# A fused two-layer gated transformer block on one core: token-tile attention, 512-column query products and a reordered head

## The chip, the cores and the metric

The kernel runs on one core of a Trainium2 chip. The metric is the device time of one execution in microseconds (us), the median of several runs. Five engines work side by side: PE (matrix multiply; its weight loads are shown as PEld), DVE (vector), ACT (scalar activation functions), POOL (GpSimd) and SP, which here only starts the transfers. They order their work by semaphores: each engine has one queue and stops at a wait until another engine has counted high enough.

## What is computed

x is [4, 256, 512] (1024 tokens of width 512), the context is [4, 64, 512]. Cut to what matters:

```python
x = x + tanh(g_xattn[0]) * xattn0(layernorm(x), ctx)   # 32 query heads, 8 key heads, keys: the 64 context rows
x = x + tanh(g_ffn[0])   * ffn0(layernorm(x))          # SiLU gate, inner width 1376
x = x + tanh(g_xattn[1]) * xattn1(layernorm(x), ctx)   # 32 query heads, 8 key heads, q and k RMS-normalised
x = x + tanh(g_ffn[1])   * ffn1(layernorm(x))          # dense base + top-2 of 28 rank-8 experts
# xattn1(latents, context):
kv = concat([context, latents], axis=1)                # 64 + 256 = 320 keys
q = rms_norm(heads(latents @ Wq), q_norm_w); k = rms_norm(heads(kv @ Wk), k_norm_w); v = heads(kv @ Wv)
out = softmax(q @ k.T / sqrt(128)) @ v                 # per head of width 128
return heads_joined(out) @ Wo
```

## The kernel before

**Split products.** Each fp32 operand is held as a rounded part (`_hi`) and a remainder (`_lo`), and every product is three matmuls: hi x lo, lo x hi, hi x hi (`mm3`, L55 to L59, so most PE rows carry L57, L58 or L59). Each result that is used again leaves PSUM in two steps: ACT writes the rounded part, DVE subtracts it from PSUM for the remainder.

**Stages.** The program runs one after the other: a head (L312 and on, until about 38 us in), `attn0_phase` over 8 key-head groups, `ffn0_phase`, `attn1_phase` over 8 groups, and inside its `tail` the last feed-forward stage. The head loads the context (`ctxT`), the first key-value, query and output weights (`raw_kv`, `raw_q`, `raw_o`), splits them (DVE rounds and subtracts, L332 to L352; POOL does the context remainder and four pieces of the output weight remainder), makes the keys and values (`kv` preps), the products of keys and query weights (`wk` preps) and the layer norm of eight token tiles (DVE statistics, POOL reciprocal root, ACT `act_norm`, PE transpose `pe_turn`, ACT `act_hi`, DVE `dve_lo`). After it POOL splits the next group's key-value weights (`split_kv`) before it first scales attention weights, and PE transposes those.

**Second attention.** A unit is one key head with its four query heads (group g, 0 to 7) and one batch row b (0 to 3): 32 units, n = 4 g + b. Each engine has the loop over b written out by hand in `body`. For unit n PE makes, in this order, keys and values (`kv_proj`, two token tiles), for even b the context's keys and values of two batch rows (`cx`), then for the unit before, u = n - 1, the products of attention weights and values (`p_v`) and transposes (`turn`), and for n the query product (`q_proj`), the transposes of k and q, the scores in four pieces, and the output product of u (`out`). PSUM has two bank pairs for this, by turns (`x_bank`, `y_bank`), so a product often waits until DVE has read the bank's former content: `p_v` of an even b waits for `kv_split`, the query product of an even b for `cx_split`.

In the query product the output tile is two heads of both token tiles: 256 columns a matmul. `PAIRS` gives the order of the score pieces. On DVE, `kv_lo` does the remainder of v (L1082), for b = 0 two pieces of the query weight remainder for this group (L1015), the remainder of the context's v (L1091) and the sums of squares of k (L1097), from which POOL makes the scale that `k_raw` gets at L1117 (`k_scaled`); `t_lo` of piece 2 (L1026) stands ahead of it.

**Late layer-norm tiles.** Six token tiles of a layer norm are made within units 1, 30 and 31 (`ln_tiles`), because x is complete only then. `turn_2` transposes the second of a pair and then piece 2 of the attention weights, which waits for `dve_lo` of the first.

## Time and profile before

| | |
|---|---|
| median of 3 runs | 1440.13 us (1435.58 to 1440.22) |
| the profiled execution | 1438.7 us, of it span 1436.9 us |
| PE busy | 1385.1 us (96%), 8744 matmuls |
| DVE busy | 1042.7 us (73%) |
| ACT busy | 796.3 us (55%) |
| POOL busy | 501.3 us (35%) |
| mean granted PE clock | 0.990 of full speed |

The span runs from the first to the last instruction; the rest of the execution's time lies around it. Matmuls overlap in the records, so a busy PE is not a measure of how fast it works: the distance from one start to the next is.

### The profile page before, as it was taken

To read this page: it belongs to the slowest core of one execution; us is meant where nothing else is said; L and a number is where in the kernel's file an instruction comes from. 1 tells how busy PE (TensorE), PEld (TensorE's weight loads), DVE (VectorE), ACT (ScalarE), POOL (GpSimd) and SP (SyncE) were. 2 spreads that over 40 slices of the span, in tenths; PEclk is the share of its full clock that TensorE was granted. 3 is DMA by queue.
4 is the path that set the end of the run, shared out by engine and by line. 5 is a ranking of instruction groups with operands and counts; after the bars stand their busy time and mean duration, and the time that the engine had idled before them with its cause. 6 is when DMAs were issued, how large, how long until landed. Compare 5 with 4: busy or idle time off the path is not lost.

```text
span 1436.9 us, 25319 instructions
## 1 busy us (share of the span) xinstructions
PE 1385.1 (96%) x8744; PEld 1240.6 (86%) x8744; DVE 1042.7 (73%) x2730; ACT 796.3 (55%) x2210; POOL 501.3 (35%) x623
## 2 busy tenths in 40 slices
PE   4999999999999998999999999999999999999998
PEld 4899989987778877899899999999999999999877
DVE  7777787787623435777787787787787777778775
ACT  4787787774211304565565565565555556556631
POOL 3965565654955512221212212222122221222220
PEclk9999999999999998999999999999999999999999
DMA  5211222211321300100100101001001001000001
GB/s 198 74 62 56 73 73 73 73 59 59 105 59 49 123 1 1 74 1 1 74 1 4 70 0 58 15 0 73 0 0 73 0 0 73 15 31 14 1 8 52
DMA packets 14944, 63.86 MB, mean 44 GB/s; under 512 B 1760, under 2 KB 1760, under 8 KB 10656
## 3 DMA queue, kind: packets, MB, share of 16 engines
q1 hardware_dynamic: 14880, 63.07, 12.5%
q8 instruction: 32, 0.52, 0.2%
q14 instruction: 32, 0.26, 0.1%
HBM read 60.97 MB, written 2.10 MB: 44 GB/s over the span
## 4 chain that ended last, share of the span: by engine, by line
PE 52%; DVE 6%; ACT 3%; issue 1%; POOL 0%; ACTq 0%
PE psum L57 15%; PE psum L58 14%; PE psum L59 14%; PE psum L1393 3%; PE psum L1406 2%; PE psum L1432 2%; ACT p L1256 1%; DVE pT_lo L1022 1%; DVE mx L1059 1%; ACT pT_hi L1231 1%; DVE pT_hi L1026 1%; PE psum L1388 1%; DVE p L1075 1%; PE psum L1509 1%; DVE v_lo L1082 0%
## 5 line engine op out<-in xcount | busy, mean ns | idle before, releaser
L1256 ACT ACTIVATE p<-psum,nb,rq 128x320 f32<-128x320 f32 x256 | 155.3, 614 | 154.5 <-DVE nb L1063 154.5
L57 PE MATMUL psum<-w1q_hi,xnT_lo 128*128 128x256 f32 (+1 forms) x544 | 163.0, 300 | 0.0
L59 PE MATMUL psum<-w1q_hi,xnT_hi 128*128 128x256 f32 (+1 forms) x544 | 157.3, 289 | 0.0
L58 PE MATMUL psum<-w1q_lo,xnT_hi 128*128 128x256 f32 (+1 forms) x544 | 157.1, 289 | 0.0
L982 POOL TENSOR_TENSOR p<-p,rinv 128x640 f32<-128x640 f32 x64 | 80.2, 1254 | 206.0 <-DVE rinv L1069 206.0
L1059 DVE TENSOR_REDUCE mx<-psum 128x2 f32<-128x640 f32 x128 | 104.7, 818 | 4.5 <-PE psum L59 4.5
L1231 ACT ACTIVATE pT_hi<-psum 128x512 fp32r<-128x512 f32 x128 | 69.7, 596 | 66.0 <-PE psum L1393 66.0
L1022 DVE TENSOR_TENSOR pT_lo<-psum,pT_hi 128x512 fp32r<-128x512 f32 x128 | 85.3, 687 | 27.7 <-ACT pT_hi L1231 25.9
L59 PEld LDWEIGHTS psum<-w1q_hi,xnT_hi 128*128 128x128 f32 x544 | 103.8, 191 | 1.3
L57 PEld LDWEIGHTS psum<-w1q_hi,xnT_lo 128*128 128x128 f32 x544 | 104.1, 191 | 1.1
L58 PEld LDWEIGHTS psum<-w1q_lo,xnT_hi 128*128 128x128 f32 x544 | 104.1, 191 | 1.0
L58 PE MATMUL psum<-w1o_lo,oT_hi 128*128 128x512 f32 x256 | 100.3, 392 | 0.0
L57 PE MATMUL psum<-w1o_hi,oT_lo 128*128 128x512 f32 x256 | 100.3, 392 | 0.0
L59 PE MATMUL psum<-w1o_hi,oT_hi 128*128 128x512 f32 x256 | 99.8, 390 | 0.0
L370 DVE TENSOR_TENSOR VW_lo<-psum,VW_hi 64x512 fp32r<-64x512 f32 x128 | 88.0, 688 | 14.5 <-ACT VW_hi L462 12.8
L57 PE MATMUL psum<-kT_hi,qT_lo 128*128 128x320 f32 x256 | 86.5, 338 | 2.3 <-DVE qT_lo L1053 2.1
L57 PE MATMUL psum<-w_kv_hi,xnT_lo 128*128 128x256 f32 x288 | 86.0, 299 | 1.8 <-PEq L692 1.8
L1046 DVE CUSTOM_DVE_ANT_0 dump<-q_raw 128x128 f32<-128x128 f32 x256 | 59.5, 288 | 34.5 <-ACT q_raw L1244 34.5
L1244 ACT ACTIVATE q_raw<-psum 128x512 f32<-128x512 f32 x64 | 38.2, 597 | 82.5 <-PE psum L59 82.4
L58 PE MATMUL psum<-w_kv_lo,xnT_hi 128*128 128x256 f32 x288 | 83.0, 288 | 0.0
L59 PE MATMUL psum<-w_kv_hi,xnT_hi 128*128 128x256 f32 x288 | 82.9, 288 | 0.0
L995 POOL TENSOR_TENSOR rq<-ssq,rms_eps 128x8 f32<-128x8 f32 x32 | 6.4, 200 | 218.8 <-DVE ssq L1046 218.8
(236 smaller groups left out, 4707.9 us busy)
## 6 DMA issues: line engine op xcount, KB each, us to landing
raw_q<-in_w0q SPq DMA_DIRECT2D x8, 1024.0 KB, 4.8
raw_o<-in_w0o SPq DMA_DIRECT2D x8, 1024.0 KB, 4.7
raw_q<-in_w1q SPq DMA_DIRECT2D x8, 1024.0 KB, 7.5
raw_o<-in_w1o SPq DMA_DIRECT2D x8, 1024.0 KB, 4.8
raw_kv<-in_w_gu SPq DMA_DIRECT2D x10, 512.0 KB, 3.6
raw_gu<-in_w_gu SPq DMA_DIRECT2D x10, 512.0 KB, 3.6
raw_kv<-in_w0kv SPq DMA_DIRECT2D x8, 515.0 KB, 3.3
raw_kv<-in_w1kv SPq DMA_DIRECT2D x8, 512.0 KB, 5.5
```

The lines of the kernel that those rows point to most:

```text
L57: pe.matmul(out, w[1], m[0], start=start, stop=False)
L58: pe.matmul(out, w[0], m[1], start=False, stop=False)
L59: return pe.matmul(out, w[0], m[0], start=False, stop=stop)
L370: last = dve.tensor_tensor(k.VW[1][r, h // 2, 2 * pr + bp, :], bank[64 * bp:64 * bp + 64, :], f(k.VW[0][r, h // 2, 2 * pr + bp, :]), ALU.s ...
L982: pool.tensor_tensor(p, p, k.rinv[:, stat(j)].unsqueeze(2).to_broadcast([PART, 2, KEYS]), ALU.mult).then_inc(p_scaled_pool, 1)
L1022: last = dve.tensor_tensor(k.pT[1][:, kt, 2 * hp:2 * hp + 2, :], bank.rearrange("p (h q) -> p h q", h=2), f(k.pT[0][:, kt, 2 * hp:2 * hp + ...
L1046: last = dve.tensor_tensor_reduce(k.dump[:, 4 * hp + i, :], q, q, 1.0, 0.0, ALU.mult, ALU.add, k.ssq[:, 4 * hp + i:4 * hp + i + 1])
L1059: dve.tensor_reduce(k.mx[:, stat(j)], s_pair(j), AX.X, ALU.max).then_inc(mx_ready, 1)
L1231: last = act.activation(k.pT[0][:, kt, 2 * hp:2 * hp + 2, :], bank.rearrange("p (h q) -> p h q", h=2), ACT.Copy)
L1244: act.activation(k.q_raw[:, hp, :], y_bank(b, "q", hp, alone)[:, :], ACT.Copy).then_inc(q_copied, 1)
L1256: last = act.activation(k.p1[:, tile, 2 * hp + hh, :], s_pair(j)[:, hh, :], ACT.Exp, bias=k.nb[:, i:i + 1], scale=k.rq[:, i:i + 1], accum_ ...
L1393: last = pe.transpose(bank[:, (2 * hh + tile) * PART:(2 * hh + tile + 1) * PART], k.p1[:, tile, 2 * hp + hh, CTX * hh + kt * PART:CTX * hh ...
```

## The change

- **Second attention by token tile.** The tiles of q, of the attention weights and of their product with v are laid out as [token tile, four heads] in place of [two heads, both tiles]. `q_proj` now makes four heads of one token tile: 12 matmuls of 512 columns in place of 24 of 256. `PAIRS` goes through the two head pairs of tile 0 first. `out` waits for its own tile's product alone.
- **Even units on DVE.** `kv_lo` is taken apart. For even b the remainder of v comes ahead of `t_lo` piece 2; then the sums of squares of k (which wait for a new semaphore, `kc_copied`), for b = 0 the two query weight pieces, and last the remainder of the context's v.
- **Unit 0.** The second query product stands behind the transposes of k; the keys and values of b = 1 are made in two halves around score piece 2, and score piece 3 stands ahead of the transposes.
- **Layer-norm units and tail.** The second late tile is transposed between the two halves of `kv_proj`, and piece 2 of the attention weights behind the second half; ACT does `act_hi` of the first tile ahead of the exponentials of piece 3. In the tail `pe_ag(0)` and `pe_base(0)` move ahead.
- **Head.** ACT rounds the key-value and query weights in pieces, DVE subtracts piece by piece and also does the context remainder; POOL rounds the output weights, the first piece between layer-norm tiles 6 and 7. The `wk` preps run over c for the first head pair and then for the second, one tile ahead of the transposes. The load of `bo` moves behind all others, `gates` and `normw` behind the query weights.

```diff
@@ second attention, views and PE
-    PAIRS = [(0, 0), (1, 0), (0, 1), (1, 1)]
+    PAIRS = [(0, 0), (0, 1), (1, 0), (1, 1)]
...
-            def q_proj(n, b, hp, alone=False):
-                for tile in range(2):
-                    t = 2 * b + tile
-                    for c in range(CH):
-                        last = mm3(pe, y_bank(b, "q", hp, alone)[:, tile * 256:(tile + 1) * 256],
-                                   [w[:, c, t * PART:(t + 1) * PART] for w in k.xnT],
-                                   [w[:, c, hp * 256:(hp + 1) * 256] for w in k.w_q], c == 0, c == CH - 1)
+            def q_proj(n, b, tile, alone=False):
+                t = 2 * b + tile
+                for c in range(CH):
+                    last = mm3(pe, y_bank(b, "q", tile, alone)[:, :], [w[:, c, t * PART:(t + 1) * PART] for w in k.xnT],
+                               [w[:, c, :] for w in k.w_q], c == 0, c == CH - 1)
                 last.then_inc(q_full, 1)
...
+                kv_half(b, 0)
+                late = ln_tiles(u)
+                if prev and not late:
+                    turn(u, b, 2)
+                if prev and late:
+                    pe.wait_ge(t_split, 6 * u + 2)
+                    ln.pe_turn(pe, *late[1], ln_bank(b - 1, 1))
+                kv_half(b, 1)
+                if prev and late:
+                    turn(u, b, 2, late=late[0])
...
                     if prev:
                         pe.wait_ge(t_split, 6 * u + 4)
-                    else:
-                        pe.wait_ge(cx_split, 1)
-                        q_proj(n, b, 1, True)
                     pe.wait_ge(k_scaled, n + 1)
...
+                    else:
+                        pe.wait_ge(cx_split, 1)
+                        q_proj(n, b, 1, True)
                     q_turn(n, b, 0, not prev)
...
                     if not prev:
-                        kv_proj(g, 1, False, False)
+                        kv_half(1, 0)
...
                     if prev:
                         out(u, b, 1)
+                    else:
+                        kv_half(1, 1)
+                        scores(n, b, 3)
                     turn(n, b, 0)
                     turn(n, b, 1)
-                    scores(n, b, 3)
+                    if prev:
+                        scores(n, b, 3)
...
             def tail(n):
                 u = n - 1
-                turn_2(u, 0)
+                late = ln_tiles(u)
                 ffn1.pe_ag(pe, 0)
+                pe.wait_ge(t_split, 6 * u + 2)
+                ln.pe_turn(pe, *late[1], ln_bank(BATCH - 1, 1))
+                turn(u, 0, 2, late=late[0])
+                ffn1.pe_base(pe, 0)
@@ second attention, DVE body
+                    if b % 2 == 0:
+                        v_lo(g, b)
+                    if prev:
                         t_lo(u, b, 2)
+                    if b % 2 == 1 and not (first and b == 1):
+                        v_lo(g, b)
                     if not (first and b == 1):
-                        kv_lo(g, b, first)
+                        k_squares(g, b)
+                    if b == 0 and not first:
+                        w_lo("q", g, 2)
+                        w_lo("q", g, 3)
+                    if b % 2 == 0:
+                        cx_lo(g, b)
                     if prev:
                         t_lo(u, b, 3)
                         t_lo(u, b, 4)
@@ head, DVE
-        head_kv()
-        head_q()
-        dve.wait_ge(in_small, 48)
+        dve.wait_ge(ctx_hi, 1)
+        dve.tensor_tensor(k.ctxT[1][:, :], k.xn_tok[:, :, :].rearrange("p a b -> p (a b)"), f(k.ctxT[0][:, :]),
+                          ALU.subtract).then_inc(ctx_lo, 1)
+        dve.wait_ge(kv_in, 16)
+        bias_copy(dve).then_inc(bias_in, 1)
+        for i in range(CONV["kv"]):
+            head_kv_lo(i)
+        head_q_row()
+        for h in range(3):
+            head_q_shift(h)
+        head_q_lo(0)
+        head_q_shift(3)
+        head_q_lo(1)
+        prep(None, ("kv", 0))
+        stats(0)
+        head_q_lo(2)
+        head_q_lo(3)
@@ head, POOL
         for t in range(NT):
             ln.pool_rstd(pool, 0, t)
-        for i in range(CONV["o"]):
+            if t == 6:
+                pool.wait_ge(o_in, 16)
+                hi_piece("o", 0)
+                lo_piece("o", 0, 0)
+        for i in range(1, CONV["o"]):
+            hi_piece("o", i)
             lo_piece("o", 0, i)
```

Where DVE starts a unit with b = 0 of groups 1 to 7, its queue before holds these rows (pT is the transposed attention weights, v_lo 128x256 the remainder of v, v_lo 64x128 that of the context's v, ssk the sums of squares of k, w1q the query weights):

```order
L1026 TENSOR_TENSOR pT_hi<-psum,pT_hi 64x256 x2
L1082 TENSOR_TENSOR v_lo<-psum,v_hi 128x256
L1015 TENSOR_TENSOR w1q_lo<-raw_q,w1q_hi 128x512 x2
L1091 TENSOR_TENSOR v_lo<-psum,v_hi 64x128 x4
L1097 ISA dump,ssk<-k_raw 128x128
...
L1022 TENSOR_TENSOR pT_lo<-psum,pT_hi 128x512 x2
```

And now, with the new kernel's line numbers:

```order
L1118 TENSOR_TENSOR v_lo<-psum,v_hi 128x256
L1065 TENSOR_TENSOR pT_hi<-psum,pT_hi 64x2x128 x2
L1125 ISA dump,ssk<-k_raw 128x128
...
L1054 TENSOR_TENSOR w1q_lo<-raw_q,w1q_hi 128x512 x2
L1133 TENSOR_TENSOR v_lo<-psum,v_hi 64x128 x4
L1061 TENSOR_TENSOR pT_lo<-psum,pT_hi 128x512 x2
```

The remainder of v has moved to the front; the remainder of the context's v, which frees the bank of the query product, now stands behind the squares as well as behind the query weight pieces.

In the head, DVE's queue before up to the first statistics of x (ln_st):

```order
L419 CAST ctxT_hi<-xn_tok 128x1024
L206 COPY bias<-raw_kv 128x6
L332 CAST w_kv_hi<-raw_kv 128x1024
L334 TENSOR_TENSOR w_kv_lo<-raw_kv,w_kv_hi 128x1024
L209 TENSOR_SCALAR q_last<-raw_q 128x4
L341 COPY raw_q<-bias 128x4
L343 TENSOR_SCALAR raw_q<-raw_q,q_last 128x511 x4
L346 CAST w0q_hi<-raw_q 128x2048
L348 TENSOR_TENSOR w0q_lo<-raw_q,w0q_hi 128x2048
L425 SCALAR_TENSOR_TENSOR qkw<-normw 128x1
L360 SCALAR_TENSOR_TENSOR kvT_lo<-psum,bias,kvT_hi 128x256 x2
L91 BN_STATS ln_st<-x 128x6
```

And now:

```order
L418 CAST ctxT_hi<-xn_tok 128x1024
L420 TENSOR_TENSOR ctxT_lo<-xn_tok,ctxT_hi 128x1024
L207 COPY bias<-raw_kv 128x6
L335 TENSOR_TENSOR w_kv_lo<-raw_kv,w_kv_hi 128x512 x2
L210 TENSOR_SCALAR q_last<-raw_q 128x4
L342 COPY raw_q<-bias 128x4
L345 TENSOR_SCALAR raw_q<-raw_q,q_last 128x511 x3
L351 TENSOR_TENSOR w0q_lo<-raw_q,w0q_hi 128x512
L345 TENSOR_SCALAR raw_q<-raw_q,q_last 128x511
L351 TENSOR_TENSOR w0q_lo<-raw_q,w0q_hi 128x512
L359 SCALAR_TENSOR_TENSOR kvT_lo<-psum,bias,kvT_hi 128x256
L91 BN_STATS ln_st<-x 128x6
```

Both big casts have left this queue, half of the query remainder and the second kvT_lo stand behind the first statistics, and the context remainder has come in.

## Rows read from the trace of the kernel before

**Rows 1.** The page, its first line.

```profile
span 1436.9 us, 25319 instructions
```

**Rows 2.** Stretches: us, busy time by engine, granted PE clock, DMA share, GB/s.

```profile
549.50:556.30 6.80, 6.18 (x27) 5.79 (x26) 4.43 (x13) 2.97 (x8) 1.85 (x2) 0.50 0.00 0
751.00:803.00 52.00, 51.73 (x348) 47.45 (x349) 41.06 (x123) 30.16 (x80) 10.77 (x12) 1.00 0.13 51
```

**Rows 3.** Timeline of PE, unit 10: start, length, what; query and output product.

```profile
805.31 0.28 PE L58 MATMUL psum<-w1q_lo,xnT_hi 128*128 128x256 f32 x1
...
807.95 0.28 PE L59 MATMUL psum<-w1q_hi,xnT_hi 128*128 128x256 f32 x1
...
815.97 0.39 PE L57 MATMUL psum<-w1o_hi,oT_lo 128*128 128x512 f32 x1
...
818.48 0.39 PE L59 MATMUL psum<-w1o_hi,oT_hi 128*128 128x512 f32 x1
```

**Rows 4.** Timeline at the start of unit 12 (b = 0), last row unit 10.

```profile
852.42 0.86 DVE L1026 TENSOR_TENSOR pT_hi<-psum,pT_hi 64x256 fp32r<-64x256 f32 x2
852.48 0.38 ACT L1270 ACTIVATE v_hi<-psum 128x256 fp32r<-128x256 f32 x1
853.31 0.42 DVE L1082 TENSOR_TENSOR v_lo<-psum,v_hi 128x256 fp32r<-128x256 f32 x1
853.65 1.28 DVE L1015 TENSOR_TENSOR w1q_lo<-raw_q,w1q_hi 128x512 fp32r<-128x512 f32 x2
853.86 0.49 PE L57 MATMUL psum<-pT_hi,v_lo 128*128 128x512 f32 x1 [0.27 <-DVE v_lo L1082]
854.95 1.20 DVE L1091 TENSOR_TENSOR v_lo<-psum,v_hi 64x128 fp32r<-64x128 f32 x4
856.17 0.29 DVE L1097 CUSTOM_DVE_ANT_0 dump<-k_raw 128x128 f32<-128x128 f32 x1
856.60 0.36 PE L57 MATMUL psum<-w1q_hi,xnT_lo 128*128 128x256 f32 x1
...
803.46 1.20 DVE L1091 TENSOR_TENSOR v_lo<-psum,v_hi 64x128 fp32r<-64x128 f32 x4 [1.22 <-ACT v_hi L1276]
```

**Rows 5.** Timeline ahead of the scores of unit 10.

```profile
813.28 0.69 DVE L1053 TENSOR_TENSOR qT_lo<-psum,qT_hi 128x512 fp32r<-128x512 f32 x1
814.12 0.39 PE L57 MATMUL psum<-kT_hi,qT_lo 128*128 128x320 f32 x1
```

**Rows 6.** Timeline in unit 0 and at the start of unit 1.

```profile
541.73 1.20 DVE L1091 TENSOR_TENSOR v_lo<-psum,v_hi 64x128 fp32r<-64x128 f32 x4 [1.87 <-ACT v_hi L1276]
...
549.12 0.83 PE L1432 MATMUL psum<-ident,q_raw 128*128 128x128 f32 x4 [2.22 <-DVE kT_lo L1136]
...
564.65 0.79 PE L57 MATMUL psum<-pT_hi,v_lo 128*128 128x512 f32 x1 [0.84 <-DVE pT_lo L1022]
```

**Rows 7.** Timeline of PE behind units 30 and 31: turns of piece 2 and of the late tile.

```profile
1343.68 0.44 PE L1388 MATMUL psum<-ident,p 128*128 128x128 f32 x2 [1.04 <-DVE xnT_lo L132]
...
1370.58 0.66 PE L120 MATMUL psum<-ident,xn_tok 128*128 128x128 f32 x4 [1.28 <-DVE pT_lo L1022]
```

**Rows 8.** Timeline of the head and the first steps behind it.

```profile
10.96 0.17 DVE L209 TENSOR_SCALAR q_last<-raw_q 128x4 f32<-128x4 f32 x1 [1.58 <-DMA raw_q<-in_w0q]
...
14.35 2.29 DVE L348 TENSOR_TENSOR w0q_lo<-raw_q,w0q_hi 128x2048 fp32r<-128x2048 f32 x1
...
17.41 0.69 DVE L91 BATCH_NORM_STATS2 ln_st<-x 128x6 f32<-128x512 f32 x1
...
34.95 5.06 POOL L246 TENSOR_TENSOR w0o_lo<-raw_o,w0o_hi 128x512 fp32r<-128x512 f32 x4 [2.09 <-DVE w0o_hi L352]
...
36.58 0.68 DVE L365 TENSOR_TENSOR WK_lo<-psum,WK_hi 128x512 fp32r<-128x512 f32 x1
...
43.76 0.64 POOL L295 TENSOR_TENSOR p<-p,rinv 128x256 f32<-128x256 f32 x1
44.45 0.44 PE L575 MATMUL psum<-ident,p 128*128 128x128 f32 x2 [0.37 <-POOL p L295]
```

More of the change, by code:

```diff
@@ L160, in attn0_phase @@
     LN_TILES = 4
-    HEAD_ORDER = [("kv", 0), ("kv", 1)] + [("wk", j) for j in range(8)] + [("vw", 0, 0)]
+    HEAD_WK = [("wk", 2 * c + hp) for hp in range(2) for c in range(CH)]
+    HEAD_ORDER = [("kv", 0), ("kv", 1)] + HEAD_WK + [("vw", 0, 0)]
     CONV = {"kv": 2, "q": 4, "o": 4}
@@ L535, in prep @@
                     pe.wait_ge(prep_free, place(base, ("kv", 0))[0] + 1)
-                    pe.wait_ge(q_lo, CONV["q"] * (g + 1))
+                    if base is not None:
+                        pe.wait_ge(q_lo, CONV["q"] * (g + 1))
+                if base is None and c == 0:
+                    pe.wait_ge(q_lo, 2 * hp + 2)
                 for h in range(2):
@@ L931, in p_pair, with shared @@
         return k.p1[:, tile, 2 * hp:2 * hp + 2, :].rearrange("p h n -> p (h n)")
+    def shared(w, tile, half, i):
+        return w[halves[half], 2, tile, i:GH:2, :]
     def stat(j):
@@ L1076, in scale_p, with v_lo @@
                 last.then_inc(p_scaled, 1)
-            def kv_lo(g, b, first):
-                n = BATCH * g + b
-                dve.wait_ge(kv_hi, n + 1)
+            def v_lo(g, b):
+                dve.wait_ge(kv_hi, BATCH * g + b + 1)
                 bank = y_bank(b, "kv")[:, :].rearrange("p (t n) -> p t n", t=2)
@@ L1083, in kv_lo, with k_squares @@
                                   ALU.subtract).then_inc(kv_split, 1)
-                if b == 0 and not first:
-                    w_lo("q", g, 2)
-                    w_lo("q", g, 3)
+            def k_squares(g, b):
                 if b % 2 == 0:
-                    dve.wait_ge(cx_hi, 2 * g + b // 2 + 1)
-                    for i in range(2):
-                        for half in (slice(0, 64), slice(64, PART)):
-                            last = dve.tensor_tensor(k.v[1][half, b + i, 2, :],
-                                                     y_bank(b, "cx")[64 * i:64 * i + 64, HD:2 * HD],
-                                                     f(k.v[0][64 * i:64 * i + 64, b + i, 2, :]), ALU.subtract)
-                    last.then_inc(cx_split, 1)
-                nk = 3 if b % 2 == 0 else 2
-                for i in range(nk):
+                    dve.wait_ge(kc_copied, 2 * g + b // 2 + 1)
+                for i in range(3 if b % 2 == 0 else 2):
                     last = dve.tensor_tensor_reduce(k.dump[:, 2 * GH + i, :], k.k_raw[:, i, :], k.k_raw[:, i, :], 1.0, 0.0,
@@ L1099, in kv_lo, with cx_lo @@
                 last.then_inc(ssk_ready, 1)
+            def cx_lo(g, b):
+                dve.wait_ge(cx_hi, 2 * g + b // 2 + 1)
+                for i in range(2):
+                    for half in (slice(0, 64), slice(64, PART)):
+                        last = dve.tensor_tensor(k.v[1][half, b + i, 2, :],
+                                                 y_bank(b, "cx")[64 * i:64 * i + 64, HD:2 * HD],
+                                                 f(k.v[0][64 * i:64 * i + 64, b + i, 2, :]), ALU.subtract)
+                last.then_inc(cx_split, 1)
             def body(g, first, nxt):
@@ L1154, in body @@
                     scale_p(n, 1)
+                    row_max(n, 2)
                     if not prev:
-                        kv_lo(g, 1, first)
-                    row_max(n, 2)
+                        v_lo(g, 1)
+                        k_squares(g, 1)
                     if prev:
@@ L1460, in kv_proj @@
                     pe.wait_ge(x_added, 2 * (u - 1) + 1)
-                for tile in range(2):
-                    t = 2 * b + tile
-                    for c in range(CH):
-                        last = mm3(pe, y_bank(b, "kv")[:, tile * 256:tile * 256 + 256],
-                                   [w[:, c, t * PART:(t + 1) * PART] for w in k.xnT],
-                                   [w[:, c, :] for w in w_kv3], c == 0, c == CH - 1)
-                    if tile == 0 and prev:
-                        turn_2(u, b)
-                last.then_inc(kv_full, 1)
+                kv_half(b, 0)
[8 more added lines that the diff above has]
+                    turn(u, b, 2, late=late[0])
             def body(g, first, nxt):
@@ L1478, in body @@
                     else:
-                        turn_2(u, b)
+                        turn(u, b, 2)
                     if deep:
```

255 lines of the change are left out of this document (127 added, 128 removed).

## Prediction

> **What bounds the kernel now.** I read the page first: PE is busy 96% of a span of 1436.9 us [rows 1], so a change counts only by what it takes from PE's own work, or from PE's waits. The windows next: in 52 us of the steady second attention PE is busy for 51.73 at full clock, the other engines for less; near the start of that stage there are 6.8 us at half the clock [rows 2]. PE works at two levels there, 2.4 GHz and 1.2 GHz, and each microsecond of full-clock work done at the lower one costs a second one. Last came the timeline, for the places at which PE waits: for DVE at the start of each even unit [rows 4], in unit 0 and at the start of unit 1 [rows 6], behind the late layer-norm tiles and in the tail [rows 7], and all through the head, whose end is a chain of DVE, POOL and PE [rows 8]. Ahead of the scores nothing is shown as a wait, but little is missing: the second q remainder starts at 813.28 with 0.69 of work, and the scores start 0.2 later than its end [rows 5]. The sum below is made against the profiled execution's own 1438.7 us, which is 1.4 below the median of the runs shown (1440.13).
>
> **Query products.** From the first to the last of 24 matmuls of 256 columns is 22 steps of the printed rows, 2.64 us, so 0.120 each; the out product's 512-column ones go 2.51 us in 11 steps, 0.228 each [rows 3]. A q product is thus 24 x 0.120 = 2.88 before and 12 x 0.228 = 2.74 now, 0.14 less. There are 64 of them. Those of units 30 and 31 meet waits for the layer norm, and unit 0 is counted below, so 60 x 0.14 = **-8.4**. The bounds: 0, if the gain only turns into waits (a rival below), and 9.0 for all 64. The transposes, scores and output products keep their shapes.
> The Trainium skill, "TensorE: Matmul & The Clock Gate", section "Back-to-back issue gap", gives an isolated matmul of N columns N/2.4 + 2.5 ns, by which dropping half the matmuls saves only the 2.5 ns of each of the 768 dropped, 1.9 us. By that rule the q term would be 1.9 us instead of 8.4. The trace does not agree with so small a fixed part: its rows [rows 3] fit one of about 12 ns.
>
> **Even units, b = 2.** p_v waits for the remainder of v. ACT's v_hi ends at 852.86, but DVE is in t_lo piece 2 until 853.28 and does the remainder at 853.31; the matmul comes at 853.86 with 0.27 of idle shown [rows 4]. With v_lo ahead of t_lo piece 2 the remainder can start 0.45 earlier; the idle by the modelled ends is 0.27, so the gain lies between these, and I take 0.4, since the modelled end of the matmul before lies behind its real share. The context's remainder is late by nothing: in unit 10 it stands after 1.22 us of idle for ACT's v_hi [rows 4], and t_lo (0.86) goes before that idle anyway, while three squares of about 0.25 fit into it. Seven of eight such units have the wait: 7 x 0.4 = **-2.8** (1.9 to 3.2).
>
> **Even units, b = 0, groups 1 to 7.** The same 0.4 is gained at p_v, but what is late next is the q product, which waits for the context's remainder (it frees the bank). DVE after v_hi's end at 852.86 now has v_lo 0.42, t_lo piece 2 0.86, three squares 0.72, two query weight pieces 1.28, and the context's remainder 1.20 [rows 4]: 4.48, so it ends at about 857.35, and q can't start before 857.4. It started at 856.60 [rows 4]. So each of these units loses 0.8 where it should have gained 0.4: PE stands for about 1.2 us. 7 x 0.8 = **+5.6**. The bounds: -2.8, if PE comes to the q product no sooner than DVE is done (it would have to be behind for another reason), and +7 if the squares have to wait for ACT's copy of the context's keys as well. What is queued behind on DVE (t_lo pieces 3 and 4, the q squares) has slack against PE, which is late itself.
>
> **Head.** DVE was free at 9.38, waited 1.58 for the query weights, and started their shift at 10.96; the first statistics came at 17.41, 6.45 later [rows 8]. Of this row the cast of the query weights goes to ACT (1.2 by half the width's rate of the 2.29 remainder [rows 8]), half the remainder (1.15) and the second kvT_lo (0.45) go behind the first statistics: 2.85 less, 3.6 left. Ahead of it, the cast of the key-value weights (another 1.2) is replaced by the context's remainder, which runs before those weights land, so DVE is free at about 8.3. The query weights now travel ahead of bo's 256 KB and two small loads; I take it that they land by then (2.6 earlier; at worst not at all earlier). First statistics: 8.3 + 3.6 = 11.9, 5.5 earlier. The layer norm then goes at its pace of eight tiles, so that the last WK remainder comes at about 31.5 instead of 36.58 [rows 8]. POOL before began its four remainders at 34.95, behind DVE's cast at t = 5, and took 5.06 [rows 8]; now it must also round the pieces, so about 1.9 for both of a piece. It does the first within the tiles and three from 28.9 on: done at about 34.6 where it was 40.0. From there to POOL's first scaled p is 3.76 (34.95 + 5.06 to 43.76), and PE turns it at 44.45 [rows 8]; the new turn is at about 39.0, **-5.4**. Bounds: -2.9 with no earlier weights, -7 if POOL's pieces overlap the rstd chain fully. This cover is thin: if POOL's casts take longer than 1.2 a piece, each 0.3 more costs 0.9 at the end.
>
> **Unit 0 and unit 1.** The sums of squares stood behind the context's remainder (1.20), which itself stood after 1.87 of idle [rows 6]; now they fit into this idle, so the scaled keys come about 2.0 earlier. The second q product (2.75), which stood ahead of the transposes of k, now fills the 2.22 us for which PE waited for kT_lo [rows 6]. Taken together PE gets to the scores min(2.22, 2.0 with 0.75 of it lost to waiting for the keys without the q product in front), about 1.5, earlier. After that wait the clock was at half for 6.8 us [rows 2], a cost of up to 3.4; an idle of 1.04 elsewhere [rows 7] is short of the one that stands before this drop, so I take half of it as recovered, 1.7. Of the 0.84 ahead of unit 1's p_v [rows 6] the new order of halves, scores and turns should take 0.5. Sum **-3.7** (-2 to -5.5).
>
> **Layer-norm units and tail.** The piece-2 turn behind the late tile waits 1.04 for the first tile's remainder [rows 7]; at unit 2 it is the same pattern. The second half of the keys and values (about 1.4 us) now lies between, so both waits go, with what hangs on them 1.2 each: **-2.4** (-1.5 to -3). In the tail 1.28 of waiting for pT_lo [rows 7] is filled by pe_ag(0), but pe_base(0) comes to its operands about as much sooner than they are ready; I take **-1.5** (0 to -3).
>
> **Sum.** -8.4 - 2.8 + 5.6 - 5.4 - 3.7 - 2.4 - 1.5 = -18.6; 1438.7 - 18.6 = 1420.1, and with 1.4 for the median about **1421**.
>
> **Rivals.**
> *The steady stretch gives its saving back (0.12).* The scores have 0.2 us of slack [rows 5]. A q product that ends sooner and the first out product that now needs its tile's p_v alone may only move PE to a wait for qT_lo or the ACT copies. For it: this slack and DVE's 47.45 of 52 busy [rows 2]. Against it: 0.28 per unit is a small part of a unit. All of the 8.4 lost: 1429.5.
> *The b = 0 wait does not come (0.14).* If ACT's v_hi and k copies come earlier than I have them, or PE is behind for another reason, the +5.6 becomes -2.8: 1412.5.
> *The head's gain does not carry (0.08).* POOL may be slower at rounding, or the weights no earlier: the head then gives 0, 1426.5.
> *512 columns give no more than the rows' differences in noise (0.04).* 0.120 against 0.228 are both read from one unit; if the saving is a fifth of it, 1.9 us in all, the time is 1427.5. The skill's formula above would give this case.
> *Slower: the clock falls in the even units (0.03).* The new stall of 1.2 us at the q product stands in 7 units, and after a stall of 2.22 the clock was at half for 6.8 us [rows 2, 6]. If each stall brought 3.4 us at half clock, 1.7 lost, the 7 give 1421 + 12 = 1433; if all 15 even units behind unit 0 stall so, 26 more make it 1447, and that is slower by 0.5%. Above the time of before it is from 12 drops on. Against it: the waits of 1.04 and 1.28 [rows 7] are like the new ones.
> The rest, 0.59, is my forecast with sizes off.
>
> **How the numbers follow.** The forecast alone holds 1415 to 1427. The range reaches to the b = 0 rival below (1412.5, and head or unit 0 a bit better than taken: 1410) and to the steady-stretch rival and half the clock drops above: **1410 to 1432**. Half a per cent, 7.2 us, is about what a measurement of this kernel can tell from no change; faster than 1432.9 is faster. All but the slower rival lie there on their own, but two rivals can come together (steady stretch and head: 1435): faster 0.89, same 0.08, slower 0.03.
>
> **What would show it.** In the new trace: 7976 matmuls instead of 8744, and q rows of 512 columns 0.228 apart; in seven units a wait of about 1.2 before the q product, released by DVE's context remainder; no wait at p_v in even units; the first turn behind the head at about 39; the scores of unit 0 about 1.5 sooner after the stage's start, and less half clock; no wait of about 1 before the piece-2 turns at units 2 and 31. What would make me wrong: a wait ahead of the scores or exponentials in each unit; POOL reaching the first scaling no earlier; a granted clock below 0.985 in the attention stage.

## The result, and the profile after

The changed kernel takes 1426.58 us (median of 4 runs, 1424.52 to 1427.87) where the kernel before, on the same chip, takes 1439.11 (4 runs). The ratio is 0.9922, with a 95% interval of 0.9905 to 0.9939: 0.8% less. Measured once more beside the kernel before (e5 below), the changed kernel gave 0.9938 (0.9923 to 0.9953). The forecast was 1421, with a range of 1410 to 1432.

The page of the changed kernel, its first and PE's line, where [rows 1] stands for before:

```profile
span 1426.1 us, 23791 instructions
...
PE 1377.5 (97%) x7976; PEld 1195.4 (84%) x7976; DVE 1040.2 (73%) x2732; ACT 799.9 (56%) x2216; POOL 506.6 (36%) x626
```

There are 768 matmuls fewer, as computed. Two rows of PE's list of waits belong to the change (waited for, total in us, times, longest):

```profile
PE psum L57 <- DVE v_lo L1133: 7.3, 7, 1.2
...
PE psum L57 <- DVE w1q_lo L1054: 2.6, 1, 2.6
```

The first row is the forecast wait at the seven b = 0 units; the second was not in the forecast's sum. The timeline around the start of unit 12 (b = 0), ACT, DVE and PE, against [rows 4]:

```profile
841.78 0.38 ACT L1316 ACTIVATE v_hi<-psum 128x256 fp32r<-128x256 f32 x1
...
842.19 0.42 DVE L1118 TENSOR_TENSOR v_lo<-psum,v_hi 128x256 fp32r<-128x256 f32 x1 [0.50 <-ACT v_hi L1316]
...
842.64 0.86 DVE L1065 TENSOR_TENSOR pT_hi<-psum,pT_hi 64x256 fp32r<-64x256 f32 x2
...
842.74 0.49 PE L57 MATMUL psum<-pT_hi,v_lo 128*128 128x512 f32 x1
...
844.17 1.29 DVE L1054 TENSOR_TENSOR w1q_lo<-raw_q,w1q_hi 128x512 fp32r<-128x512 f32 x2
...
845.50 1.19 DVE L1133 TENSOR_TENSOR v_lo<-psum,v_hi 64x128 fp32r<-64x128 f32 x4
...
846.74 0.50 PE L57 MATMUL psum<-w1q_hi,xnT_lo 128*128 128x512 f32 x1 [1.02 <-DVE v_lo L1133]
```

The product of weights and values starts with no wait, 0.1 behind the remainder of v. From v_lo to the end of the context's v_lo DVE is busy without a gap, 842.19 to 846.69, and the query product starts 0.05 later. The query product itself, from its second to its last matmul, against [rows 3]:

```profile
795.15 0.39 PE L58 MATMUL psum<-w1q_lo,xnT_hi 128*128 128x512 f32 x1
...
797.46 0.39 PE L59 MATMUL psum<-w1q_hi,xnT_hi 128*128 128x512 f32 x1
797.69 0.49 PE L1544 MATMUL psum<-ident,k_raw 128*128 128x128 f32 x3
```

These are ten steps of 0.231. The first matmul, at 794.82, takes 0.33 to the second. So the product is 2.87 long, from its start to the start of what follows, where it was 2.96 before.

The head, against [rows 8] (query weights' arrival, statistics, the last WK remainder, POOL's last output weight piece, its first scaled p, the first turn):

```profile
8.35 0.17 DVE L210 TENSOR_SCALAR q_last<-raw_q 128x4 f32<-128x4 f32 x1 [0.65 <-DMA raw_q<-in_w0q]
...
11.81 0.69 DVE L91 BATCH_NORM_STATS2 ln_st<-x 128x6 f32<-128x512 f32 x1
...
27.60 0.68 DVE L364 TENSOR_TENSOR WK_lo<-psum,WK_hi 128x512 fp32r<-128x512 f32 x1
...
33.29 1.30 POOL L247 TENSOR_TENSOR w0o_lo<-raw_o,w0o_hi 128x512 fp32r<-128x512 f32 x1
...
38.32 0.63 POOL L296 TENSOR_TENSOR p<-p,rinv 128x256 f32<-128x256 f32 x1
...
40.98 0.38 PE L607 MATMUL psum<-ident,p 128*128 128x128 f32 x2
```

The turn is PE's first transpose of attention weights behind the head. DVE's first statistics, POOL's last piece and its first scaled p are where they were forecast (11.9, 34.6, 38.3), but the turn stands at 40.98 and no longer waits for POOL. A window shows why, and another shows the same thing behind the tail's wait (us, busy by engine, granted clock):

```profile
31.00:38.00 7.00, 6.29 (x24) 5.63 (x24) 3.96 (x7) 4.39 (x15) 6.84 (x9) 0.51 0.34 110
1361.80:1366.30 4.50, 4.42 (x12) 3.53 (x13) 2.39 (x10) 0.00 (x0) 0.00 (x0) 0.62 0.00 0
```

In both PE works at about half the clock, behind waits (2.46 for tile 7, up to 29.73, and 2.65 in the tail).

### The profile page after: what moved, and what is told of

Same layout as the page of the kernel before. It is cut to its first block, busy times and chain, and to the rows that moved or that the text cites. A ratio compares the mean times of both kernels' runs of the same rounds, so it can differ in the third digit from the quotient of the medians.

```text
span 1426.1 us, 23791 instructions
## 1 busy us (share of the span) xinstructions
PE 1377.5 (97%) x7976; PEld 1195.4 (84%) x7976; DVE 1040.2 (73%) x2732; ACT 799.9 (56%) x2216; POOL 506.6 (36%) x626
## 3 DMA queue, kind: packets, MB, share of 16 engines
q1 hardware_dynamic: 14880, 63.07, 12.5%
## 4 chain that ended last, share of the span: by engine, by line
PE 55%; DVE 5%; ACT 2%; issue 1%; POOL 0%; DVEq 0%; ACTq 0%
PE psum L57 16%; PE psum L59 15%; PE psum L58 15%; PE psum L1436 3%; PE psum L1447 2%; PE psum L1468 2%; PE psum L1431 1%; DVE w1q_lo L1054 1%; DVE v_lo L1133 1%; DVE pT_hi L1065 1%; PE psum L1544 1%; DVE pT_lo L1061 0%; ACT p L1302 0%; DVE dump L1125 0%; PE psum L120 0%
## 5 line engine op out<-in xcount | busy, mean ns | idle before, releaser
L57 PE MATMUL psum<-w1q_hi,xnT_lo 128*128 128x512 f32 x288 | 120.2, 417 | 10.0 <-DVE v_lo L1133 7.3
L59 PE MATMUL psum<-w1q_hi,xnT_hi 128*128 128x512 f32 x288 | 114.0, 396 | 0.0
L58 PE MATMUL psum<-w1q_lo,xnT_hi 128*128 128x512 f32 x288 | 112.9, 392 | 0.0
L1291 ACT ACTIVATE q_raw<-psum 128x512 f32<-128x512 f32 x64 | 38.3, 599 | 85.4 <-PE psum L59 85.3
L473 ACT ACTIVATE VW_hi<-psum 64x512 fp32r<-64x512 f32 x128 | 76.0, 594 | 9.7 <-PE psum L59 7.7
L497 ACT ACTIVATE p<-psum,nb 128x64 f32<-128x64 f32 x256 | 76.9, 318 | 7.4 <-DVE nb L398 7.0
L59 PE MATMUL psum<-kT_hi,qT_hi 128*128 128x320 f32 x256 | 79.1, 309 | 0.0
```

Of the source, the lines that this page charges most:

```text
L57: pe.matmul(out, w[1], m[0], start=start, stop=False)
L58: pe.matmul(out, w[0], m[1], start=False, stop=False)
L59: return pe.matmul(out, w[0], m[0], start=False, stop=stop)
L473: last = act.activation(k.VW[0][r, h // 2, 2 * pr + bp, :], bank[64 * bp:64 * bp + 64, :], ACT.Copy)
L497: last = act.activation(k.p0[:, s % 4, h * CTX:(h + 1) * CTX], s_bank[s % 2][:, h * CTX:(h + 1) * CTX], ACT.Exp, bias=k.nb0[:, s % 2, h:h ...
```

## The experiments

Eleven kernels ran in three groups: e1 to e4, e5 to e8, and e9 to e11. The first and the third ran on one chip, the second on another. The kernel before ran beside each group (medians 1435.46, 1435.86 and 1436.40), and each ratio is to it. For most questions the profiles tell more than the medians. They are cut into stages by PE's own rows: the first turn behind the head; the first key product of the second attention ("start"); the first product of weights and values of unit 1; the key products that start units 3 and 31; the last matmul. The columns "turn" and "start" are times from the span's start; each of the four behind them is the length from one mark to the next. "Pads" are two memsets of POOL in the tail.

| | turn | start | unit 0 | to unit 3 | units 3 to 30 | unit 31 to end | span |
|---|---|---|---|---|---|---|---|
| before, first profile | 44.45 | 534.35 | 30.30 | 53.40 | 722.48 | 92.78 | 1436.9 |
| before, second (e11) | 44.59 | 534.55 | 26.52 | 52.57 | 722.33 | 92.00 | 1431.6 |
| changed, first profile | 40.98 | 531.33 | 24.80 | 52.07 | 720.57 | 93.70 | 1426.1 |
| changed, second (e5) | 38.89 | 529.17 | 24.82 | 51.39 | 720.36 | 92.09 | 1421.4 |
| head alone (e7) | 38.94 | 529.09 | 26.53 | 52.49 | 722.24 | 92.01 | 1426.0 |
| 256 columns (e4) | 38.82 | 528.66 | 24.93 | 51.68 | 726.05 | 93.49 | 1428.4 |
| old even units (e6) | 40.30 | 530.45 | 28.29 | 51.64 | 716.86 | 93.66 | 1424.5 |
| old tail (e2) | 40.90 | 530.75 | 24.80 | 53.90 | 720.32 | 91.16 | 1424.6 |
| o pieces last (e3) | 39.51 | 529.40 | 24.81 | 51.35 | 720.33 | 94.83 | 1424.3 |
| q pieces on POOL (e1) | 39.19 | 529.07 | 24.81 | 51.35 | 712.42 | 92.54 | 1413.8 |
| same, pads first (e9) | 40.18 | 530.66 | 24.81 | 51.36 | 712.58 | 89.21 | 1412.2 |
| same, head split (e10) | 41.24 | 531.07 | 26.31 | 51.40 | 712.40 | 89.17 | 1413.9 |
| e1 with old tail and e3 (e8) | 39.79 | 530.17 | 26.30 | 51.38 | 712.69 | 91.04 | 1415.2 |

**The query weight pieces on POOL (e1).**

```diff
@@ DVE, body
-                    if b == 0 and not first:
-                        w_lo("q", g, 2)
-                        w_lo("q", g, 3)
@@ DVE, tail
-                w_lo("q", NKV, 2)
-                w_lo("q", NKV, 3)
@@ POOL, body, behind p_scale(n, 2)
+                    if b == BATCH - 1:
+                        for i in (2, 3):
+                            src, hi, lo = weights("q", g + 1, i)
+                            pool.wait_ge(whi["q"], CONV["q"] * (g + 1) + i + 1)
+                            pool.tensor_tensor(lo, src, f(hi), ALU.subtract).then_inc(wlo["q"], 1)
```

> The two query weight remainder pieces of each b = 0 unit (1.28 us of DVE) and of the tail are made by POOL behind its second scaling in b = 3, where POOL is idle for 6 us; DVE is left without them. Theory (what stands in DVE's queue ahead of the context's v remainder sets the q product's start): the seven waits of 1.0 to 1.2 us before the q product at b = 0 go, 7 x 1.05 = 7.4, and the tail's wait of 2.65 for the second piece goes with the half-clock stretch behind it (1.7), some 3 of it in the end: 1426.6 - 10.5 = about 1416 (1413 to 1419). Rival (the wait only moves on, to the scaled keys, whose POOL and DVE chain ends 0.9 us before PE needs it now): half of the 7.4, about 1420. Rival (POOL beside DVE slows DVE's own work through shared access to memory): no gain, 1424 or more, and longer DVE rows around POOL's.

1415.63, ratio 0.9861 (0.9847 to 0.9876). The timeline ahead of unit 12's query product, POOL, DVE and PE:

```profile
832.94 2.56 POOL L1043 TENSOR_TENSOR w1q_lo<-raw_q,w1q_hi 128x512 fp32r<-128x512 f32 x2
...
839.08 1.20 DVE L1138 TENSOR_TENSOR v_lo<-psum,v_hi 64x128 fp32r<-64x128 f32 x4
...
840.33 0.50 PE L57 MATMUL psum<-w1q_hi,xnT_lo 128*128 128x512 f32 x1
...
840.74 1.29 DVE L1066 TENSOR_TENSOR pT_lo<-psum,pT_hi 128x512 fp32r<-128x512 f32 x2 [0.47 <-ACT pT_hi L1279]
```

The wait is gone at all seven units, and units 3 to 30 are 7.9 shorter (720.36 to 712.42), where 7.4 was expected. The scaled keys do not take the wait over: DVE now even stands 0.47 for ACT before t_lo. While POOL makes its pieces (832.94 to 835.50) DVE's remainder from PSUM keeps its 0.68, and a small row between buffers takes 0.30 where it takes 0.16 alone; that is all that the second rival finds, and both rivals fall. The tail did not give its 3 us, since POOL's pieces now stood ahead of memsets that PE needs:

```profile
1347.57 0.39 PE L57 MATMUL psum<-w_kv_hi,xnT_lo 128*128 128x256 f32 x1 [1.75 <-POOL w_kv_lo L1696]
```

**The tail in its old order (e2).**

```diff
@@ PE, tail; DVE and ACT are put back likewise
+                pe.wait_ge(t_split, 6 * u + 2)
+                ln.pe_turn(pe, *late[1], ln_bank(BATCH - 1, 1))
+                turn(u, 0, 2, late=late[0])
                 ffn1.pe_ag(pe, 0)
-                pe.wait_ge(t_split, 6 * u + 2)
-                ln.pe_turn(pe, *late[1], ln_bank(BATCH - 1, 1))
-                turn(u, 0, 2, late=late[0])
-                ffn1.pe_base(pe, 0)
...
                 ffn1.pe_ag(pe, 1)
+                ffn1.pe_base(pe, 0)
                 turn(u, 0, 5)
```

> Only the tail is put back to the order before (late layer norm turn, piece-2 turn, then pe_ag(0); pe_base(0) behind pe_ag(1)), on PE, DVE and ACT. Theory (the tail's part of the change costs time, since pe_base(0) comes to the query weight remainder 2.65 us early and the clock falls behind that wait): 2 to 2.5 faster than the changed kernel, about 1424.3. Rival (the loss comes from the late tiles and the turns, which any order meets: before had waits of 1.28 and 1.29 and a half clock too): no difference, 1426.6.

1425.63, ratio 0.9930 (0.9917 to 0.9942), which does not tell it from the changed kernel. In the profile the last stretch is 91.16, against 93.70 and 92.09 in the two of the changed kernel. So the new tail costs 0.9 us, or 2.5 where the clock falls too. The other order has its own waits, 1.28 at the second late tile and 1.32 in p_v.

**POOL's output weight pieces behind tile 7 (e3).**

```diff
-            if t == 6:
-                pool.wait_ge(o_in, 16)
-                hi_piece("o", 0)
-                lo_piece("o", 0, 0)
-        for i in range(1, CONV["o"]):
+        pool.wait_ge(o_in, 16)
+        for i in range(CONV["o"]):
```

> POOL takes all four output weight pieces behind layer norm tile 7, none between 6 and 7. Theory (in the changed head PE, and no longer POOL, sets the first turn: the last tile is late by 1.9 and PE then runs 6 us at half the clock): tile 7 is normalised at 27.0 instead of 28.86, the first turn stands 1 to 1.9 earlier, time about 1425.2. Rival (POOL's first scaled p, at 38.3 now, sets it as before): POOL's row of pieces ends 0.5 later, the turn 0 to 0.5 later than now if it was POOL that counted; 1426.6 to 1427.

1426.12, ratio 0.9934 (0.9921 to 0.9947): no gain. The timeline of PE, which is still waiting, only elsewhere:

```profile
28.32 0.66 PE L120 MATMUL psum<-ident,xn_tok 128*128 128x128 f32 x4 [1.05 <-ACT xn_tok L111]
...
29.47 0.47 PE L57 MATMUL psum<-w0o_hi,kvT_lo 128*128 128x512 f32 x1 [0.49 <-POOL w0o_lo L247]
...
31.38 0.47 PE L57 MATMUL psum<-w0o_hi,kvT_lo 128*128 128x512 f32 x1 [0.98 <-POOL w0o_lo L247]
...
39.51 0.44 PE L604 MATMUL psum<-ident,p 128*128 128x128 f32 x2 [1.67 <-POOL p L296]
```

The tile is on time, and this head kept the full clock from 7 to 48 us, yet PE meets POOL at the turn. Here the rival was right: PE stands 1.67 for POOL's scaled p, so POOL sets the turn.

**256 columns in the new layout (e4).**

```diff
-                for c in range(CH):
-                    last = mm3(pe, y_bank(b, "q", tile, alone)[:, :], ..., [w[:, c, :] for w in k.w_q], ...)
+                for half in range(2):
+                    cols = slice(half * 256, (half + 1) * 256)
+                    for c in range(CH):
+                        last = mm3(pe, y_bank(b, "q", tile, alone)[:, cols], ..., [w[:, c, cols] for w in k.w_q], ...)
```

> The query product is again 24 matmuls of 256 columns (two heads each), in the new layout; all else as in the changed kernel. Theory (saving per product is the distance from the start of a product to what follows, 2.96 against 2.87, so 0.09 to 0.10, since the first matmul of a row costs more at 512 columns and the 512 column steps are 0.231): + 60 x 0.095 = 5.7, about 1432.3. Rival (0.14 each, as forecast, with part of it lost to waits): +3 to +4 in units where PE waits anyway and the rest 8.4: 1435. Rival (only 2.5 ns a dropped matmul): +1.9, 1428.5.

1432.68, ratio 0.9977 (0.9967 to 0.9986), about 0.5% above the changed kernel. Units 12 to 15 last 27.53, 24.81, 26.32 and 24.81, in the changed kernel 27.34, 24.63, 26.11 and 24.63: 0.2 each, 0.10 a product, 5.7 over units 3 to 30. The odd units are back to the 24.82 of before, so nothing else of the change shows in them.

**The changed kernel again (e5).** No edit.

> The changed kernel once more, on the chip of these runs, as a yardstick. Ratio to before 0.992. Its units should repeat those of its first profile to 0.03 us each (27.33, 24.63, 26.11, 24.62 for b = 0 to 3). Theory (the head's PE stretch at half the clock behind the wait for layer norm tile 7 differs from execution to execution): the first turn lies anywhere between 38.8 and 41.0. Rival (the first turn is set by POOL's scaled p): always at 38.8 to 39.2, with a wait for POOL.

1427.54, ratio 0.9938. Every stage repeats, apart from those with a half-clock stretch. The turn stands at 38.89, and so close behind POOL's first scaled p that the two meet:

```profile
38.22 0.62 POOL L296 TENSOR_TENSOR p<-p,rinv 128x256 f32<-128x256 f32 x1
...
38.89 0.45 PE L607 MATMUL psum<-ident,p 128*128 128x128 f32 x2
```

The tail has the same wait without the fall. The timeline of PE at it:

```profile
1358.85 0.50 PE L57 MATMUL psum<-w1q_hi,xnT_lo 128*128 128x512 f32 x1 [2.64 <-DVE w1q_lo L1054]
```

And the window behind it, as long as that shown of the first profile:

```profile
1358.80:1363.30 4.50, 4.45 (x19) 3.68 (x20) 2.36 (x9) 0.00 (x0) 0.00 (x0) 1.00 0.00 0
```

**DVE's old order in even units (e6).**

```diff
-                    if b % 2 == 0:
-                        v_lo(g, b)
                     if prev:
                         t_lo(u, b, 2)
-                    if b % 2 == 1 and not (first and b == 1):
+                    if not (first and b == 1):
                         v_lo(g, b)
-                    if not (first and b == 1):
-                        k_squares(g, b)
...
                     if b % 2 == 0:
                         cx_lo(g, b)
+                    if not (first and b == 1):
+                        k_squares(g, b)
```

> DVE's order in even units is that of before (t_lo piece 2, v remainder, query weight pieces, context's v remainder, squares), all else as changed. Theory (the reorder costs 0.87 in each b = 0 unit and gives 0.33 in each b = 2 unit, and PE's waits follow DVE's queue alone): b = 0 units 26.46 us instead of 27.33, b = 2 units 26.44 instead of 26.11; over the stage 6.1 less and 2.3 more, and unit 0 loses up to 2 as the squares go behind the context's remainder again: 2 to 4 faster than the changed kernel, ratio to before 0.990. Rival (some of the 0.87 is due to the token tile layout, not the order): b = 0 units stay above 27, no gain or a loss, 0.994.

1426.26, ratio 0.9927 (0.9912 to 0.9942). Units of b = 0 last 26.43 and of b = 2 26.44, as expected to 0.03: the order alone costs 0.9 at b = 0 and gives 0.33 at b = 2. Units 3 to 30 win 3.5 us by it. Unit 0 is 3.5 longer (28.29 against 24.82), but only 2.0 of that is the order: PE waits for the scaled keys.

```profile
541.79 0.55 PE L1542 MATMUL psum<-ident,k_raw 128*128 128x128 f32 x3 [2.38 <-DVE k_raw L1162]
```

In the changed kernel this wait is 0.40. The other 1.5 is the clock's: from 530 to 535 us it was granted at 0.66. A like stretch at the start of unit 0 makes this stage 1.5 longer in e8 and e10 too (26.30 and 26.31), and there the squares stand as in the changed kernel. So by its stages the old order is 1.5 the faster one, and the 2 to 4 that were expected did not come.

**The head alone (e7).** The kernel before, with every hunk of the diff that lies in the head.

> The kernel before with the changed head alone. Theory (the head is worth 5.4, of which a half-clock stretch takes up to 2 back in some executions): first turn between 38.8 and 41.0 instead of 44.45, ratio to before 0.9965 (0.996 to 0.998), the stages behind it as long as before. Rival (the head's gain is lost behind it, in the first attention's waits for POOL or for loads): ratio 0.999 to 1.

1429.53, ratio 0.9952 (0.9937 to 0.9968). The turn is at 38.94, 5.65 earlier than in e11; the other stages are those of e11 within 0.1, apart from 0.2 that is lost between the turn and the start. The ratio is a little lower than expected (0.996 to 0.998). Which part of the new head gives how much (the loads, ACT's casts, the order of the wk preps) was not taken apart.

**POOL's pieces, old tail, e3's head (e8).**

```diff
@@ as e1, but in the last group POOL makes its pieces in the tail
+                ffn1.pool_weights(pool)
+                q_pieces(NKV)
@@ and the edits of e2 and e3
```

> The changed kernel with the query weight pieces 2 and 3 on POOL (those of the tail behind POOL's own work for the last stage), the old order of the tail, and POOL's output weight pieces behind layer norm tile 7. Theory (b = 0 waits and the tail's loss are both due to DVE's pieces; in the old tail order p_v's last two matmuls waited 1.32 for a t_lo that stood behind them): b = 0 units 26.2, the stretch from unit 31's start to the last matmul 90 us or less where it is 93.7 in the changed kernel and 92.5 with POOL's pieces alone; ratio to before 0.984. Rival (the tail is bound elsewhere): the last stretch stays at 91.2 or more, ratio 0.986.

1416.79, ratio 0.9863 (0.9845 to 0.9880): no better than e1. The last stretch is 91.04. The theory on the tail is wrong: p_v's last two matmuls still wait, 1.23, although the pieces are gone from DVE.

```profile
1355.07 0.50 PE L1448 MATMUL psum<-pT_hi,v_lo 128*128 128x512 f32 x1 [1.23 <-DVE pT_hi L1071]
```

**New tail with the pieces in time (e9).**

```diff
@@ as e1, but in the last group, with the memsets taken out of pool_weights
+                ffn1.pool_pad(pool)
+                q_pieces(NKV)
                 ffn1.pool_weights(pool)
```

> The changed kernel with the query weight pieces 2 and 3 on POOL, in the tail behind POOL's two memsets (for which PE waited 1.75 in the first such kernel) and ahead of its other work; head and tail order as changed. Theory (the tail's loss in the changed kernel is the wait of 2.65 for the second piece, nothing else in its order): b = 0 units 26.2, and from unit 31's start to the last matmul at most 90.5 (92.1 to 94.8 with the wait, 91.0 to 91.2 in the old order). Ratio to before 0.984. Rival (the new order of the tail has another wait behind this one, for DVE's late tile or a PSUM bank): 91.5 or more, ratio 0.986.

1415.07, ratio 0.9854 (0.9838 to 0.9869), the fastest of all by its median and by its profile's span (1412.2), if not clear of e1. The last stretch is 89.21, 2.9 less than in e5, with neither the wait of 2.6 nor that of 1.75. The new order is the better one, once the pieces are there.

**The head with DVE sharing the pieces (e10).**

```diff
@@ POOL, on top of e9
-            if t == 6: ...
+        for i in range(CONV["o"]):
+            hi_piece("o", i)
+        pool.wait_ge(o_lo, 2)
+        for i in range(2, CONV["o"]):
+            lo_piece("o", 0, i)
@@ DVE: head_o_lo(0) ahead of dve_lo of tile 7, head_o_lo(1) behind it
```

> The same, and in the head POOL rounds all four output weight pieces behind tile 7 and makes remainders 2 and 3, while DVE, idle there, makes remainders 0 and 1. Theory (two ends meet at the first turn: PE's row behind the late tile 7 and POOL's pieces, so only both together bring it forward): POOL is through at about 32 instead of 34.5, tile 7 is not late, no wait of 2.47 and no half-clock stretch behind it; first turn at 37 to 37.5 where it was 38.8 to 41. Ratio to before 0.982. Rival (DVE's pieces delay the last xnT and VW remainders, and PE stands for them): turn at 38.5 or later, no gain over the run beside it.

1415.31, ratio 0.9854: no gain. In its profile the turn is at 41.24. DVE's remainders come late, PE waits 1.36 for one, and runs at half the clock behind it; POOL stands 1.82 for DVE.

```profile
31.59 0.77 PE L57 MATMUL psum<-w0o_hi,kvT_lo 128*128 128x512 f32 x1 [1.36 <-DVE w0o_lo L339]
...
32.73 2.54 POOL L247 TENSOR_TENSOR w0o_lo<-raw_o,w0o_hi 128x512 fp32r<-128x512 f32 x2 [1.82 <-DVE w0o_lo L339]
```

The query weights also landed 1.0 later here than in e5. So the rival's outcome came, but how much of it is due to the edit stays open.

**The kernel before again (e11).** No edit.

> The kernel before once more, for a second profile of it. Theory (its first profile, with a mean granted clock of 0.990, held more half-clock stretches around the start of the second attention than others of the same kernel, and so the unit 0 term was partly that): unit 0 to the first product of weights and values about 26.5 us, as with the changed head alone, where the first profile had 30.3; first turn at 44.5 and even units at 26.67 unchanged. Rival (the stretches belong to the kernel before): 30.3 again.

1435.40, ratio 0.9997 (0.9987 to 1.0008). Unit 0 takes 26.52, not 30.30. The windows of its profile:

```profile
525.00:560.00 35.00, 27.80 (x188) 24.82 (x186) 20.87 (x63) 11.11 (x31) 5.71 (x9) 1.00 0.00 1
560.00:565.00 5.00, 3.93 (x12) 2.77 (x13) 2.67 (x8) 1.95 (x6) 3.29 (x9) 0.66 0.01 3
```

There is no half clock ahead of 560 us, where the first profile had 6.8 us of it [rows 2]. But there is some from 560 to 565, in the stage "to unit 3", where e5 has none.

## Why the forecast was right, and which of its steps were not

The fairest measure of the terms is the pair e11 and e5, one on each side, with the fewest half-clock stretches. They ran on two chips, but e7, on e5's chip, repeats e11's stages behind the start to 0.1. The spans differ by 10.2, and the stages account for it: -5.4 up to the start, -1.7 in unit 0, -1.2 to unit 3, -2.0 in units 3 to 30, +0.1 behind. The forecast sum was -18.6. The medians gave -12.5 in the first measurement and -8.3 with e5.

So the time fell into the range, but the gain was about half to two thirds of the forecast, and that the range was 22 us wide helped. The time alone proves little: three rivals stood at 1426.5, 1427.5 and 1429.5, all nearer to 1426.58 than the 1421 was. It is the stages that tell them apart. Most of what is missing lies in four terms: the query products (2.4 short), the tail (2.2), units 0 and 1 (2.0) and the layer-norm units (1.2).

- **Head (forecast -5.4): right.** The first statistics, POOL's pieces and its first scaled p came within 0.1 us of the forecast, and the turn moved by 5.65 to 5.7 (e7, e5 against e11). One step was wrong without harm: the last WK remainder came at 27.6 instead of 31.5. What the forecast missed is that PE meets POOL at the turn: a wait of 2.5 for the late tile 7 stands ahead, and some half clock follows it. Eight profiles have this head. In four (e1, e4, e5, e7; granted clock 0.83 from 28 to 38 us) the turn stands 0.05 to 0.06 behind the end of POOL's scaled p, as in the kernel before, at 38.8 to 39.2. In the other four (e2, e6, e9 and the first; clock 0.66) PE comes 1 to 2 us behind it, at 40.2 to 41.0. Moving POOL's pieces back (e3) only makes POOL the later of the two.
- **Query products (forecast -8.4): the mechanism right, the size wrong.** The step "a q product is thus 24 x 0.120 = 2.88 before and 12 x 0.228 = 2.74 now" took the pitch of the steps for the length of the product. It left out that the first matmul takes 0.33 to the next at 512 columns and 0.20 at 256 (805.11 to 805.31), and it took 0.228 from the out product where the q product has 0.231. Start to start it is 2.96 (805.11 to 808.07) and 2.87. The out product, from which 0.228 was taken, has no such longer first step: it has 0.23 from its first matmul on. e4 shows 0.10 a product, near 6 us for 60. By the rule of the Trainium skill, "TensorE: Matmul & The Clock Gate", section "Back-to-back issue gap", the isolated matmul takes N/2.4 + 2.5 ns, and the term would be 1.9 us, an estimate. The runs do not agree: e4 shows 5.7 over 28 units alone.
- **b = 2 (forecast -2.8): right.** 0.33 a unit (e4's 26.33 against 26.66 before), 2.3 in all.
- **b = 0 (forecast +5.6): right.** The forecast row of DVE, from v_hi's end to the end of the context's remainder, was 4.48; measured, from 842.16 to 846.69, it is 4.53. The order costs 0.87 a unit, 6.1 in all (e4, e6), and what it waits for is DVE's row: e1 takes 1.28 from the row and gets 1.13 a unit back.
- **Unit 0 and unit 1 (forecast -3.7): too large.** 1.7 in the clean pair. The step "I take half of it as recovered, 1.7" rested on a half-clock stretch that the profile happened to have. In the first pair of profiles this stage shows 5.5, of which 3.8 is the first profile's own clock. The part worked out from the waits, 1.5, was nearly right: the scores come 13.43 behind the start in e5 and 14.73 in e11, 1.3 sooner. e6 shows that it comes from the squares: with these put back, PE waits 2.38 for the scaled keys. The step "Of the 0.84 ahead of unit 1's p_v the new order of halves, scores and turns should take 0.5" failed: this wait is 1.09 in e11 and 1.09 in e5. What each of the moves in unit 0 gives was not tested alone.
- **Layer-norm units (forecast -2.4): half of it.** No wait is left ahead of the turns at units 2 and 31, but part of it comes back in p_v: 0.57 at unit 2 and 0.35 at unit 31, which the forecast put at nothing. e11 and e5 at unit 2:

```profile
588.75 0.44 PE L1388 MATMUL psum<-ident,p 128*128 128x128 f32 x2 [1.03 <-DVE xnT_lo L132]
...
583.69 0.50 PE L57 MATMUL psum<-pT_hi,v_lo 128*128 128x512 f32 x1 [0.57 <-DVE v_lo L1118]
```

Unit 2 is 0.6 shorter (28.04 to 27.46) and so is unit 31 (28.10 to 27.51), query products included. The other 0.6 of the stage "to unit 3" lies in unit 1, and is e11's half clock there: the changed kernel's first profile, granted 0.66 from 556 to 561 us, has no gain in that unit (24.66 from its p_v to unit 2, where e11 has 24.53).
- **Tail (forecast -1.5): the wrong sign.** The step "pe_base(0) comes to its operands about as much sooner than they are ready" let the two cancel. They do not: PE waits 2.65 there, since DVE makes both query weight pieces only behind its last scaling of attention weights. From the first late tile's turn behind unit 31 to the last matmul the tail is 0.7 longer (63.90 to 64.58). Unit 31 and the tail together should have given 2.7 and gave nothing (92.00 to 92.09); in the first pair of profiles, each with a half-clock stretch in its tail, it was a loss of 0.9 (92.78 to 93.70). e9 shows the cause: with the pieces on POOL, in time, the last stretch is 2.8 shorter than in e11 (89.21).

Of the rivals, the steady stretch did not give its saving back: the odd units keep all of their 0.2 (24.82 to 24.62). The slower one fell too: seven stalls of 1.02 to 1.18 at the b = 0 query products never brought the clock down, and in each of the two profiles of the changed kernel the seven units repeat to 0.08.

## What to carry to other kernels

When PE waits for an engine's queue, count all that stands in that queue behind the last event that releases it, and then ask which of it another engine could do while it is idle: 1.28 us of weight remainder a group, moved to an idle POOL, was worth about as much again as the whole change (ratio 0.9861 against 0.9938 and 0.9922). When a wait is taken away, look for what PE waits for next: at units 2 and 31 a third to a half of it came back one product later. A product's length is from its start to the start of what follows, not the number of its steps times the distance between them. And take a second profile of the same kernel before putting a price on a half-clock stretch.

## What the runs showed of the hardware

The same wait of PE is followed by half the clock in one execution and by the full clock in another. The tail's wait of 2.64 to 2.65 was followed by a granted clock of 0.62 over 4.5 us in one profile of the changed kernel and by 1.00 in the other. It was alike at the start of the second attention of the kernel before (0.50 over 6.8 us, or 1.00). Such stretches are worth up to 3.8 us in one stage and explain why two profiles of the same kernel differ by 5 us (1436.9 and 1431.6, 1426.1 and 1421.4) while the stages without them repeat to 0.2 us in 720. At the start of unit 0 the clock fell in e6, e8 and e10 (0.66 over 5 us) and stayed full in e5 and e9, behind the same idle of 1.84. What decides it in an execution was not found.

One small row of DVE, between SBUF tiles, is held until POOL's instruction ends. Two rows of the changed kernel's DVE, the same instruction, the first inside POOL's scaling (834.17 to 835.42), the second with POOL idle:

```profile
834.84 0.59 DVE L1100 SCALAR_TENSOR_TENSOR nb<-mx,rq 128x2 f32<-128x2 f32 x1
...
839.27 0.16 DVE L1100 SCALAR_TENSOR_TENSOR nb<-mx,rq 128x2 f32<-128x2 f32 x1
```

The first ends at 835.43, 0.01 behind POOL. In this profile 32 of the 128 rows of this kind are longer than 0.2, and each of them ends within 0.03 of the end of a POOL instruction, 31 times a scaling. In e1 the row that took 0.30 (833.96 to 834.26) ends as the first of POOL's two weight pieces does (834.24). This is not so for every row: DVE's remainders from PSUM keep their 0.68 beside POOL, and so does the output weight remainder, which stays in SBUF, beside POOL's row of 1.64 that makes a reciprocal root. It costs nothing there, as PE is not waiting for these rows.
